# One exponential per graph with a copied head, the sum scaled from PSUM, moments behind the output, and programs without loops

## The chip, the cores and the metric

The kernel runs on one core of a Trainium2 chip. The metric is the device time in microseconds. The core has five programs that run side by side and meet by semaphores: TensorE (PE), VectorE (DVE), ScalarE (ACT), GpSimd (POOL) and SyncE (SP), which issues nearly all DMAs.

## The reference

x holds 128 graphs of 128 nodes and 512 features; all share one 128 x 128 adjacency. Cut to what matters:

```python
# layer 0
h = maximum(layernorm(x), 0)
A = einsum('od,bdn->bon', adj, h);  C = A + b0[:, None]
x = x + max over the last axis of relu(A[:, :, None, :] + (C - A)[:, :, :, None])
# layer 1
h = maximum(layernorm(x), 0)
q, k, v = h @ Wq + bq, h @ Wk + bk, h @ Wv + bv          # 8 heads of 64
scores = q k^T / 8 + (-1e9 where adj == 0)
x = x + softmax(scores) @ v
```

In layer 0, C - A is b0 for every element, so the term per node is relu(max over features of A + b0): one number per graph and node, the column c. It is added to a whole row of x, so the layer norm of layer 1 is the same as that of the input, and one h serves both layers. The result is x + c + softmax(scores) v, with bv added to x, since the weights of a softmax sum to one.

## The kernel before

To keep float32 precision with float16 matmuls, each operand is split: a "head" in float16 and a "rest", the float16 of the difference. Each product is three matmuls (head x head, head x rest, rest x head).

The unit of work is a slot: in slot k every engine works on one graph in each of its steps, at offsets that are constants at the top of the file (lines 25 to 27). The order inside a slot is written out by hand, per engine, in functions named slot:

- SP: loads x of graph k+8 (L175), transposes h of graph k+5 by DMA (L198), stores y of graph k-7 (L180), transposes the probabilities of graph k-5 by DMA (L206).
- GpSimd: adds bv (L277) and the column c (L280) to x of graph k; the rest of h of graph k+5 (L268); the rest of one chunk of q or k (L289); four small operations for scale and shift of the layer norm of graph k+6 (norm_scales, L247 to L257), which wait for VectorE's moments; the rest of the probabilities of graph k-5 (L296); the rest of the second chunk (L289).
- ScalarE: the head of v (L352); the column c of graph k (L374); h of graph k+5 in float32 and float16 (L333, L334); a chunk of q or k as head and in float32 (L345, L347); two exponentials of graph k-5 (L362 into float16, L364 into float32); the second chunk.
- VectorE: for graph k-5 the masked scores (L451), the row maximum (L455) and the shift (L458); the maximum over the adjacency product of graph k+3 (L435); the rest of v of graph k-1 (L440); the statistics of graph k+6 (L417); for graph k-7 the reciprocal of the row sums (L465), its scaling (L467) and eight outputs of y (L474); the aggregate of the statistics (L427).
- TensorE: scores of graph k-5 (L660), two chunks of q or k for a group of four graphs (L631), the adjacency product of graph k+4 (L616), v of graph k (L643), probabilities x v of graph k-6 (L675).

The PSUM tile o_ps of the last product has one copy: L675 waits until y of the graph before is done (`wait(pe, y_done, m)`). So does the pair of score banks, for masked. Five graphs are left for a tail, in which VectorE alternates between shift and output (L598 to L604).

SP's program is written out for all 128 slots. The other four have eight slots straight, a loop of 14 rounds of eight slots, and eight straight:

Of the kernel before, what the change touches and what calls it, by code (L numbers as in the profile page):

```python
# [6 lines left out]
ALU = mybir.AluOpType  # L7
ACT = mybir.ActivationFunctionType
# [5 lines left out]
P = 128  # L14
# [7 lines left out]
EXP_BITS = 0x7F800000  # L22
UP_BITS = float((2 * 127 + 14) << 23)
PEAK_FLOOR = 2.0 ** -32
LOAD_AHEAD, MOMENTS_AHEAD, NORM_AHEAD, TURN_AHEAD, PREP_AHEAD, AMAX_AHEAD = 8, 6, 5, 5, 4, 3
ATTN_BEHIND, OUT_BEHIND, STORE_BEHIND = 5, 6, 7
V_BEHIND, Y_BEHIND = 1, 7
DVE_RESTS = 3
# [2 lines left out]
def graph_layers(nc, x, adj, b0, wq, bq, wk, bk, wv, bv, out):  # L31
# [6 lines left out]
    with ExitStack() as ctx:  # L38
        def sb(name, shape, dt=F32):
            return ctx.enter_context(nc.sbuf_tensor(name, shape, dt))  # L40
# [20 lines left out]
        up = sb("up", [P, 4])  # L61
        down = sb("down", [P, 4])
        undo = sb("undo", [P, 3])
        redo = sb("redo", [P, 2])
        score_scale = sb("score_scale", [P, 1])
        peak_floor = sb("peak_floor", [P, 4])
        bqk_peak = sb("bqk_peak", [P, 2])
# [4 lines left out]
        plus_minus = sb("plus_minus", [P, 2])  # L72

        x_in = sb("x_in", [P, RING, D])
        xbv = sb("xbv", [P, D])
        x1 = sb("x1", [P, RING, D])
        y = sb("y", [P, 2, D])
        stats = sb("stats", [P, 2, 6])
# [16 lines left out]
        probs = sb("probs", [P, H, P])  # L95
        probs16 = sb("probs16", [P, 2, 2, H, P], F16)
        probsT = sb("probsT", [P, 2, 2, H, P], F16)
        inv_sum = sb("inv_sum", [P, 2, H // 2])
        out_scale = sb("out_scale", [P, 2, H // 2])


# [26 lines left out]
            sem("s_ready"), sem("masked_done"), sem("max_done"), sem("shifted_done"), sem("probs_done"))  # L128
        probs_head_done, probs_rest_done = sem("probs_head_done"), sem("probs_rest_done")
        probsT_done = [sem(f"probsT_done{i}") for i in range(2)]  # L130
        o_ready, inv_sum_done, out_scale_done, y_done = sem("o_ready"), sem("inv_sum_done"), sem("out_scale_done"), sem("y_done")
        c_done, xc_done, x1_done = sem("c_done"), sem("xc_done"), sem("x1_done")

        def wait(eng, s, count):
# [19 lines left out]

        def slots(eng, slot, after_first=None):

            for k in range(RING):
                slot(0, k)
                if k == 0 and after_first:
                    after_first()  # L160
            with eng.Fori(RING, B - 2 * RING + 1, RING) as base:
                for k in range(RING):
                    slot(base, k)
            for k in range(RING):
                slot(B - RING, k)

        block = ctx.enter_context(nc.Block())

# [1 line left out]
        def _(sp):  # L170
            def load(base, k):
                if in_range(base, k):

                    wait(sp, x1_done, base + k - RING + 1)
                    sp.dma_start(x_in[:, k % RING, :], x[base + k, :, :]).then_inc(x_loaded[k % RING], 16)  # L175

            def store(base, k):
# [50 lines left out]
        def _(pool):  # L228
# [39 lines left out]
                    pool.tensor_tensor(h16[:, k % 4, 1, :], h32[:, k % 2, :], h16[:, k % 4, 0, :],  # L268
                                       ALU.subtract).then_inc(h_rest_done, 1)

            def add_c(base, k):

                if in_range(base, k):
                    m = base + k
                    wait(pool, y_done, m - RING + 1)
                    wait(pool, x1_done, m)
                    pool.tensor_tensor(xbv[:, :], x_in[:, k % RING, :], bv_rows[:, :], ALU.add).then_inc(xc_done, 1)  # L277
                    pool.wait_ge(xc_done, m + 1)
                    pool.wait_ge(c_done, m + 1)
                    pool.tensor_tensor(x1[:, k % RING, :], xbv[:, :],  # L280
                                       c_col[:, k % RING, :].to_broadcast([P, D]), ALU.add).then_inc(x1_done, 1)

            def qk_rest(base, k, u):

# [22 lines left out]

            def slot(base, k):
                u = 2 * (k % GROUP)
                add_c(base, k)  # L310
                rest(base, k + NORM_AHEAD)
                qk_rest(base, k, u)
                norm_scales(base, k + MOMENTS_AHEAD)
                probs_rest(base, k - ATTN_BEHIND)
                qk_rest(base, k, u + 1)

            slots(pool, slot)
            for graph in TAIL:
# [3 lines left out]
        def _(act):  # L322
# [33 lines left out]
            def exps(base, k):  # L356

                if in_range(base, k):
                    m = base + k
                    act.wait_ge(shifted_done, m + 1)  # L360
                    wait(act, probsT_done[k % 2], (m - k % 2) * 8)
                    nc.scalar.activation(probs16[:, k % 2, 0, :, :], shifted[:, :, :], ACT.Exp, scale=HD ** -0.5).then_inc(probs_head_done, 1)  # L362
                    wait(act, probs_rest_done, m)
                    nc.scalar.activation(probs[:, :, :], shifted[:, :, :], ACT.Exp, scale=HD ** -0.5).then_inc(probs_done, 1)  # L364

            def c_of(base, k):

                if in_range(base, k):
                    m = base + k
                    if isinstance(base, int) and m == 0:  # L370
                        act.wait_ge(down_done, 1)
                    act.wait_ge(a_evac, m + 1)
                    wait(act, x1_done, m - RING + 1)
                    nc.scalar.activation(c_col[:, k % RING, :], a_max[:, k % RING, :], ACT.Relu, scale=down[:, 3:4],  # L374
                                         bias=b0_col[:, :]).then_inc(c_done, 1)

            def w_head(j, batch):
                act.wait_ge(scale_done, batch + 1)
# [18 lines left out]
            def slot(base, k):  # L397
                u = 2 * (k % GROUP)
                v_head(base, k - 1)
                c_of(base, k)  # L400
                normalise(base, k + NORM_AHEAD)
                qk_out(base, k, u)
                exps(base, k - ATTN_BEHIND)
                qk_out(base, k, u + 1)

            slots(act, slot, after_first=lambda: w_head(1, 3))
            v_head(B, -1)
# [4 lines left out]
        def _(dve):  # L412
# [24 lines left out]
            def v_rest(base, k):  # L437
                if in_range(base, k):
# [3 lines left out]
                        proj[:, V_BANK, :].rearrange("p (h d) -> p h d", d=HD), P_SCALE,  # L442
                        v16[:, 0, k // GROUP % 2, k % GROUP, :, 0:HD], ALU.mult, ALU.subtract).then_inc(v_evac, 1)

            def softmax_shift(base, k, banks=sc):

                if in_range(base, k):
                    m = base + k
                    wait(dve, shifted_done, m)
                    dve.wait_ge(s_ready, m + 1)  # L450
                    nc.vector.scalar_tensor_tensor(masked[:, :, :], banks[:, :, :].rearrange("p t (h n) -> p (t h) n", n=P),  # L451
                                                   score_scale[:, :], mask8[:, :].unsqueeze(1).to_broadcast([P, H, P]),
                                                   ALU.mult, ALU.add).then_inc(masked_done, 1)
                    dve.wait_ge(masked_done, m + 1)
                    nc.vector.tensor_reduce(row_max[:, :], masked[:, :, :], AX.X, ALU.max).then_inc(max_done, 1)  # L455
                    dve.wait_ge(max_done, m + 1)
                    wait(dve, probs_done, m)
                    nc.vector.tensor_tensor(shifted[:, :, :], masked[:, :, :],  # L458
                                            row_max[:, :].unsqueeze(2).to_broadcast([P, H, P]), ALU.subtract).then_inc(shifted_done, 1)

            def attention_out(base, k):
                if in_range(base, k):
                    m = base + k
                    dve.wait_ge(o_ready, m + 1)
                    nc.vector.reciprocal(inv_sum[:, :, :], o_view[:, :, :, HD]).then_inc(inv_sum_done, 1)  # L465
                    dve.wait_ge(inv_sum_done, m + 1)
                    nc.vector.tensor_scalar(out_scale[:, :, :], inv_sum[:, :, :], undo[:, 2:3], None,  # L467
                                            ALU.mult).then_inc(out_scale_done, 1)
                    dve.wait_ge(out_scale_done, m + 1)
                    dve.wait_ge(x1_done, m + 1)  # L470
                    wait(dve, y_stored[k % 2], (m - k % 2) * 8)
# [41 lines left out]
            def projection_scales(j, i):  # L513
                dve.wait_ge(down_done, i + 1)
                nc.vector.tensor_scalar(undo[:, j:j + 1], down[:, j:j + 1], 1.0 / P_SCALE, None, ALU.mult).then_inc(undo_done, 1)
                if j < 2:
                    dve.wait_ge(scale_done, i + 1)
                    nc.vector.tensor_scalar(redo[:, j:j + 1], up[:, j:j + 1], H_SCALE * P_SCALE, None, ALU.mult).then_inc(redo_done, 1)
                    dve.wait_ge(redo_done, j + 1)
                    nc.vector.tensor_scalar(bqk_up[:, j, :], bqk[:, j, :], redo[:, j:j + 1], None, ALU.mult).then_inc(bias_done, 1)  # L520

            def w_rest(j, i):
# [55 lines left out]
            projection_scales(1, 3)  # L578
            dve.wait_ge(mask_done, 2)
            dve.wait_ge(undo_done, 3)  # L580

            def k_rest():

# [4 lines left out]
            def slot(base, k):  # L588
                softmax_shift(base, k - ATTN_BEHIND)
                if not isinstance(base, int) or base + k > 0:  # L590
                    adjacency_out(base, k + AMAX_AHEAD)
                v_rest(base, k - V_BEHIND)
                stats_of(base, k + MOMENTS_AHEAD)
                moments_wait(base, k + MOMENTS_AHEAD)
                attention_out(base, k - Y_BEHIND)
                moments_of(base, k + MOMENTS_AHEAD)

            slots(dve, slot, after_first=k_rest)  # L598
            v_rest(B, -V_BEHIND)
            for i, graph in enumerate(TAIL):  # L600
                softmax_shift(*graph, TAIL_BANKS[i % 3])
                attention_out(B, graph[1] - Y_BEHIND + ATTN_BEHIND)
            for k in range(-Y_BEHIND + ATTN_BEHIND, 0):
                attention_out(B, k)  # L604
# [145 lines left out]
```

## Time and profile before

| | |
|---|---|
| median of 3 runs | 1386.8 us (1386.61 to 1387.9) |
| the profiled execution | 1386.83 us |
| its span, first to last instruction | 1384.9 us |
| mean granted TensorE clock | 0.980 of full speed |
| busy: PE, DVE, ACT, POOL | 94%, 77%, 64%, 90% |
| DMA | 171.71 MB, mean 124 GB/s |
| stretch from 200 to 400 us | PE busy 194.42 us, DVE 157.31, ACT 131.52, POOL 188.33 |

Busy is the time in which an engine has an instruction in work; an instruction that is held up once it has begun counts as busy too. In the trace, a row of the timeline says when an instruction started, how long it took, and in brackets how long its engine had been idle before it and for whom.

### The profile page before, as it was taken

How to read it: one execution, taken by the hardware profiler on the slowest of the kernel's cores; microseconds unless marked ns; L12 is line 12 of the kernel's file. 1: busy time of each engine (PE TensorE's matmuls, PEld its weight loads, DVE VectorE, ACT ScalarE, POOL GpSimd, SP SyncE). 2: the span in 40 equal slices, each digit the busy share in tenths (PEclk: the TensorE clock that was granted, in tenths of full speed). 3: DMA queues.
4: the chain of work that ended last, by engine and by line, in shares of the span. 5: the costliest groups of instructions: out<-in, count | busy, mean ns of one | idle time of the engine just before them, and what ended most of it. 6: DMA issues, size and time to landing. Idle time of an engine off the chain costs nothing.

```text
span 1384.9 us, 32665 instructions
## 1 busy us (share of the span) xinstructions
PE 1304.8 (94%) x11145; PEld 676.4 (49%) x11145; DVE 1066.9 (77%) x2228; ACT 879.7 (64%) x1294; POOL 1242.3 (90%) x1288
## 2 busy tenths in 40 slices
PE   4899999999999999999999999999999999999982
PEld 1344545545455555545545455454545555455542
DVE  6458787787887887887887877878877878878777
ACT  4566666666666676666666666666766666666552
POOL 2888999999999999999999999999999999999852
PEclk8999999999999999999999999999999999999995
DMA  7244555555555565555555555555555555555445
GB/s 199 62 81 111 137 127 124 129 127 129 123 129 136 115 130 129 127 122 136 129 118 132 124 129 126 129 132 118 129 131 123 130 131 125 118 136 122 97 81 129
DMA packets 441378, 171.71 MB, mean 124 GB/s; under 512 B 406784, under 2 KB 406912, under 8 KB 441344
## 3 DMA queue, kind: packets, MB, share of 16 engines
q1 hardware_dynamic: 440000, 171.03, 55.3%
q10 hardware_dynamic: 1344, 0.27, 0.1%
q8 instruction: 16, 0.26, 0.1%
q14 instruction: 18, 0.15, 0.0%
HBM read 37.03 MB, written 33.55 MB: 51 GB/s over the span
## 4 chain that ended last, share of the span: by engine, by line
PE 75%; DVE 18%; issue 4%; DMA 1%; SPq 0%; DVEq 0%; POOL 0%; ACT 0%; POOLq 0%; ACTq 0%
PE proj L631 38%; PE proj L643 19%; PE sc L660 7%; PE o_ps L675 7%; PE proj L616 4%; DVE y L474 4%; DVE masked L451 3%; DVE row_max L455 3%; DVE out_scale L467 2%; DVE a_max L435 1%; DVE stats L417 1%; DVE v L440 1%; DVE inv_sum L465 1%; DMA x_in<-in_x 0%; DVE shifted L458 0%
## 5 line engine op out<-in xcount | busy, mean ns | idle before, releaser
L631 PE MATMUL proj<-hT,w 128*128 128x512 f16 x3072 | 689.8, 381 | 11.3 <-DMA hT<-h 6.8
L631 PEld LDWEIGHTS proj<-hT,w 128*128 128x128 f16 x3072 | 291.2, 98 | 361.0 <-issue 17.5
L643 PE MATMUL proj<-w,hT 128*128 128x512 f16 x1536 | 352.4, 379 | 1.1 <-DVE w L526 1.1
L451 DVE SCALAR_TENSOR_TENSOR masked<-sc,score_scale,mask 128x1024 f32<-128x1024 f32 x125 | 160.4, 1283 | 241.2 <-PE sc L660 241.2
L289 POOL TENSOR_TENSOR qkT<-qk,qkT 128x512 f16<-128x512 f32 x256 | 296.5, 1158 | 9.4 <-ACT qk L347 9.2
L296 POOL TENSOR_TENSOR probs<-probs 128x1024 f16<-128x1024 f32 x128 | 273.3, 2135 | 25.2 <-ACT probs L364 25.2
L345 ACT ACTIVATE qkT<-proj,bqk_up 128x512 f16<-128x512 f32 x256 | 173.4, 677 | 170.7 <-PE proj L631 170.7
L277 POOL TENSOR_TENSOR xbv<-x_in,bv_rows 128x512 f32<-128x512 f32 x128 | 276.2, 2158 | 0.0
L643 PEld LDWEIGHTS proj<-w,hT 128*128 128x128 f16 x1536 | 150.0, 98 | 182.8 <-DVE w L526 1.5
L474 DVE SCALAR_TENSOR_TENSOR y<-o_ps,out_scale,x 128x64 f32<-128x64 f32 x1024 | 208.2, 276 | 11.2
L458 DVE TENSOR_TENSOR shifted<-masked,row_max 128x1024 f32<-128x1024 f32 x128 | 189.2, 1478 | 4.4
L333 ACT ACTIVATE h<-x_in,h_add,h_mul 128x512 f32<-128x512 f32 x128 | 104.0, 813 | 110.6 <-POOL h_add L257 110.6
L347 ACT ACTIVATE qk<-proj,bqk_up 128x512 f32<-128x512 f32 x256 | 173.5, 678 | 0.0
L352 ACT ACTIVATE v<-proj 128x512 f16<-128x512 f32 x128 | 76.4, 597 | 151.1 <-PE proj L643 151.1
L362 ACT ACTIVATE probs<-shifted 128x1024 f16<-128x1024 f32 x128 | 135.3, 1057 | 48.3 <-DVE shifted L458 45.8
L675 PE MATMUL o_ps<-v,probsT 128*128 128x65 f16 (+1 forms) x3072 | 117.9, 195 | 45.3 <-DVE y L474 30.9
L455 DVE TENSOR_REDUCE row_max<-masked 128x8 f32<-128x1024 f32 x128 | 156.2, 1220 | 4.4
L675 PEld LDWEIGHTS o_ps<-v,probsT 128*128 128x128 f16 x3072 | 109.1, 99 | 85.9 <-issue 64.5
L268 POOL TENSOR_TENSOR h<-h 128x512 f16<-128x512 f32 x125 | 146.4, 1172 | 4.1 <-ACT h L334 4.1
L280 POOL TENSOR_TENSOR x<-xbv,c_col 128x512 f32<-128x512 f32 x128 | 133.8, 1045 | 10.9 <-ACT c_col L374 1.1
L364 ACT ACTIVATE probs<-shifted 128x1024 f32<-128x1024 f32 x128 | 133.2, 1041 | 0.0
L660 PE MATMUL sc<-qkT 64*128 64x128 f16 x3000 | 106.1, 218 | 5.5 <-DVE masked L451 5.5
(59 smaller groups left out, 937.6 us busy)
## 6 DMA issues: line engine op xcount, KB each, us to landing
x_in<-in_x SPq DMA_DIRECT2D x128, 256.0 KB, 2.6
out_x<-y SPq DMA_DIRECT2D x128, 256.0 KB, 2.3
hT<-h SPq DMA_TRANSPOSE x128, 3.1
probsT<-probs SPq DMA_TRANSPOSE x128, 4.3
w_raw<-in_L_gnn_Wq SPq DMA_DIRECT2D x1, 1024.0 KB, 9.2
w_raw<-in_L_gnn_Wv SPq DMA_DIRECT2D x1, 1024.0 KB, 11.4
w_raw<-in_L_gnn_Wk SPq DMA_DIRECT2D x1, 1024.0 KB, 13.4
bv_rows<-in_L_gnn_bv ACTq DMA_DIRECT2D x1, 256.0 KB, 6.8
```

The lines of the kernel that those rows point to most:

```text
L277: pool.tensor_tensor(xbv[:, :], x_in[:, k % RING, :], bv_rows[:, :], ALU.add).then_inc(xc_done, 1)
L289: pool.tensor_tensor(qk_place(k, u, 1), qk32[:, u % 2, :], qk_place(k, u, 0), ALU.subtract).then_inc(qk_rest_done, 1)
L296: pool.tensor_tensor(probs16[:, k % 2, 1, :, :], probs[:, :, :], probs16[:, k % 2, 0, :, :], ALU.subtract).then_inc(probs_rest_done, 1)
L347: nc.scalar.activation(qk32[:, u % 2, :], place, ACT.Identity, scale=P_SCALE, bias=bias).then_inc(qk_evac, 1)
L451: nc.vector.scalar_tensor_tensor(masked[:, :, :], banks[:, :, :].rearrange("p t (h n) -> p (t h) n", n=P), score_scale[:, :], mask8[:, :]. ...
L455: nc.vector.tensor_reduce(row_max[:, :], masked[:, :, :], AX.X, ALU.max).then_inc(max_done, 1)
L458: nc.vector.tensor_tensor(shifted[:, :, :], masked[:, :, :], row_max[:, :].unsqueeze(2).to_broadcast([P, H, P]), ALU.subtract).then_inc(sh ...
L474: last = nc.vector.scalar_tensor_tensor(y[:, k % 2, cols], o_view[:, h // 4, h % 4, 0:HD], out_scale[:, h // 4, h % 4:h % 4 + 1], x1[:, k ...
L631: last = nc.tensor.matmul(proj[:, u % 2, :], w16[:, j, s, c, col * P:(col + 1) * P], hT[:, k // GROUP % 2, t, c, :, :].rearrange("p g n -> ...
L643: last = nc.tensor.matmul(proj[:, V_BANK, :], hT[:, k // GROUP % 2, s, c, k % GROUP, :], w16[:, 2, t, c, :], start=(c == 0 and i == 0), st ...
L660: last = nc.tensor.matmul(banks[:, half, c * P:(c + 1) * P], qkT[rows, k // GROUP % 2, s, 0, c, k % GROUP, :], qkT[rows, k // GROUP % 2, t ...
L675: last = nc.tensor.matmul(o_view[:, h // 4, h % 4, 0:w], probsT[:, k % 2, s, h % 2 * 4 + h // 2, :], v16[:, t, k // GROUP % 2, k % GROUP, ...
```

## The change

- ScalarE makes one exponential per graph, the float32 one. The float16 head of the probabilities is a copy on VectorE (probs_head), placed behind v_rest and ahead of attention_out; GpSimd's rest follows it as before.
- The row sums are first scaled from PSUM into SBUF and the reciprocal is taken of the scaled sums. Before, the reciprocal was taken from PSUM and scaled in SBUF.
- On VectorE statistics and aggregate (stats_of, moments_of) both stand behind attention_out.
- ScalarE adds the column c to x (add_c, an Identity activation with c as bias, into the new double tile xc), at the end of its slot; GpSimd's one pass (add_bv) adds bv, at the end of its slot.
- x is loaded 7 graphs ahead, and a load waits for xc and no longer for x1.
- All programs are written out for 128 slots, without a loop.

```diff
-LOAD_AHEAD, MOMENTS_AHEAD, NORM_AHEAD, TURN_AHEAD, PREP_AHEAD, AMAX_AHEAD = 8, 6, 5, 5, 4, 3
+LOAD_AHEAD, MOMENTS_AHEAD, NORM_AHEAD, TURN_AHEAD, PREP_AHEAD, AMAX_AHEAD = 7, 6, 5, 5, 4, 3
...
-            for k in range(RING):
+            for k in range(B):
                 slot(0, k)
                 if k == 0 and after_first:
                     after_first()
-            with eng.Fori(RING, B - 2 * RING + 1, RING) as base:
-                for k in range(RING):
-                    slot(base, k)
-            for k in range(RING):
-                slot(B - RING, k)
...
-                    wait(sp, x1_done, base + k - RING + 1)
+                    wait(sp, xc_done, base + k - RING + 1)
...
-            def add_c(base, k):
+            def add_bv(base, k):
 
                 if in_range(base, k):
                     m = base + k
                     wait(pool, y_done, m - RING + 1)
-                    wait(pool, x1_done, m)
-                    pool.tensor_tensor(xbv[:, :], x_in[:, k % RING, :], bv_rows[:, :], ALU.add).then_inc(xc_done, 1)
                     pool.wait_ge(xc_done, m + 1)
-                    pool.wait_ge(c_done, m + 1)
-                    pool.tensor_tensor(x1[:, k % RING, :], xbv[:, :],
-                                       c_col[:, k % RING, :].to_broadcast([P, D]), ALU.add).then_inc(x1_done, 1)
+                    pool.tensor_tensor(x1[:, k % RING, :], xc[:, k % 2, :], bv_rows[:, :], ALU.add).then_inc(x1_done, 1)
...
                 u = 2 * (k % GROUP)
-                add_c(base, k)
                 rest(base, k + NORM_AHEAD)
                 qk_rest(base, k, u)
                 norm_scales(base, k + MOMENTS_AHEAD)
                 probs_rest(base, k - ATTN_BEHIND)
                 qk_rest(base, k, u + 1)
+                add_bv(base, k)
...
                     act.wait_ge(shifted_done, m + 1)
-                    wait(act, probsT_done[k % 2], (m - k % 2) * 8)
-                    nc.scalar.activation(probs16[:, k % 2, 0, :, :], shifted[:, :, :], ACT.Exp, scale=HD ** -0.5).then_inc(probs_head_done, 1)
                     wait(act, probs_rest_done, m)
                     nc.scalar.activation(probs[:, :, :], shifted[:, :, :], ACT.Exp, scale=HD ** -0.5).then_inc(probs_done, 1)
...
+            def add_c(base, k):
+
+                if in_range(base, k):
+                    m = base + k
+                    act.wait_ge(c_done, m + 1)
+                    wait(act, x1_done, m - 1)
+                    nc.scalar.activation(xc[:, k % 2, :], x_in[:, k % RING, :], ACT.Identity, bias=c_col[:, k % RING, :]).then_inc(xc_done, 1)
...
                 qk_out(base, k, u + 1)
+                add_c(base, k)
...
+            def probs_head(base, k):
+
+                if in_range(base, k):
+                    m = base + k
+                    dve.wait_ge(probs_done, m + 1)
+                    wait(dve, probsT_done[k % 2], (m - k % 2) * 8)
+                    nc.vector.tensor_copy(probs16[:, k % 2, 0, :, :], probs[:, :, :]).then_inc(probs_head_done, 1)
...
-                    nc.vector.reciprocal(inv_sum[:, :, :], o_view[:, :, :, HD]).then_inc(inv_sum_done, 1)
-                    dve.wait_ge(inv_sum_done, m + 1)
-                    nc.vector.tensor_scalar(out_scale[:, :, :], inv_sum[:, :, :], undo[:, 2:3], None,
-                                            ALU.mult).then_inc(out_scale_done, 1)
+                    nc.vector.tensor_scalar(scaled_sum[:, :, :], o_view[:, :, :, HD], redo[:, 2:3], None,
+                                            ALU.mult).then_inc(sum_done, 1)
+                    dve.wait_ge(sum_done, m + 1)
+                    nc.vector.reciprocal(out_scale[:, :, :], scaled_sum[:, :, :]).then_inc(out_scale_done, 1)
...
                 v_rest(base, k - V_BEHIND)
+                probs_head(base, k - ATTN_BEHIND)
+                attention_out(base, k - Y_BEHIND)
                 stats_of(base, k + MOMENTS_AHEAD)
                 moments_wait(base, k + MOMENTS_AHEAD)
-                attention_out(base, k - Y_BEHIND)
                 moments_of(base, k + MOMENTS_AHEAD)
...
                 softmax_shift(*graph, TAIL_BANKS[i % 3])
+                probs_head(*graph)
                 attention_out(B, graph[1] - Y_BEHIND + ATTN_BEHIND)
```

## Rows read from the trace of the kernel before

**Rows 1.** The page, parts 1 and 2: busy time, and the granted clock in tenths.

```profile
PE 1304.8 (94%) x11145; PEld 676.4 (49%) x11145; DVE 1066.9 (77%) x2228; ACT 879.7 (64%) x1294; POOL 1242.3 (90%) x1288
...
PEclk8999999999999999999999999999999999999995
```

**Rows 2.** The chain that ended last, shares of the span by engine.

```profile
PE 75%; DVE 18%; issue 4%; DMA 1%; SPq 0%; DVEq 0%; POOL 0%; ACT 0%; POOLq 0%; ACTq 0%
```

**Rows 3.** Timeline (start us, us, engine, line, operation), TensorE: scores of slots 8, 18, 123.

```profile
108.09 0.84 PE L660 MATMUL sc<-qkT 64*128 64x128 f16 x24
...
718.21 0.85 PE L660 MATMUL sc<-qkT 64*128 64x128 f16 x24
...
1293.99 0.84 PE L660 MATMUL sc<-qkT 64*128 64x128 f16 x24
```

**Rows 4.** Timeline of slot 8, VectorE's scaling and GpSimd's rest of h.

```profile
115.15 1.16 POOL L268 TENSOR_TENSOR h<-h 128x512 f16<-128x512 f32 x1
...
115.18 1.15 DVE L467 TENSOR_SCALAR out_scale<-inv_sum,undo 128x8 f32<-128x8 f32 x1
```

**Rows 5.** Groups by line: count, busy us, mean ns, idle before.

```profile
L467 DVE TENSOR_SCALAR out_scale<-inv_sum,undo 128x8 f32<-128x8 f32 x128 | 57.6, 450 | 4.6
```

**Rows 6.** Timeline from one y to the next, 705 to 717 us, VectorE and TensorE.

```profile
705.59 1.63 DVE L474 SCALAR_TENSOR_TENSOR y<-o_ps,out_scale,x 128x64 f32<-128x64 f32 x8
...
707.36 0.89 PE L675 MATMUL o_ps<-v,probsT 128*128 128x65 f16 x24 [0.91 <-DVE y L474]
...
708.18 0.84 PE L660 MATMUL sc<-qkT 64*128 64x128 f16 x24
...
709.07 1.28 DVE L451 SCALAR_TENSOR_TENSOR masked<-sc,score_scale,mask 128x1024 f32<-128x1024 f32 x1 [1.77 <-PE sc L660]
...
710.39 1.22 DVE L455 TENSOR_REDUCE row_max<-masked 128x8 f32<-128x1024 f32 x1
...
711.64 1.39 DVE L458 TENSOR_TENSOR shifted<-masked,row_max 128x1024 f32<-128x1024 f32 x1
...
714.15 0.68 DVE L417 BATCH_NORM_STATS2 stats<-x_in 128x6 f32<-128x512 f32 x1
...
714.86 0.21 DVE L465 RECIPROCAL inv_sum<-o_ps 128x8 f32<-128x8 f32 x1
...
715.10 0.23 DVE L467 TENSOR_SCALAR out_scale<-inv_sum,undo 128x8 f32<-128x8 f32 x1
...
715.37 1.63 DVE L474 SCALAR_TENSOR_TENSOR y<-o_ps,out_scale,x 128x64 f32<-128x64 f32 x8
```

**Rows 7.** Timeline of the tail, first and last of five shifts.

```profile
1345.14 1.22 DVE L458 TENSOR_TENSOR shifted<-masked,row_max 128x1024 f32<-128x1024 f32 x1
...
1368.80 1.22 DVE L458 TENSOR_TENSOR shifted<-masked,row_max 128x1024 f32<-128x1024 f32 x1
```

**Rows 8.** Timeline of the same slot as rows 6, GpSimd.

```profile
710.79 1.15 POOL L289 TENSOR_TENSOR qkT<-qk,qkT 128x512 f16<-128x512 f32 x1
...
711.91 2.25 POOL L277 TENSOR_TENSOR xbv<-x_in,bv_rows 128x512 f32<-128x512 f32 x1
```

**Rows 9.** Timeline of the slot before, shift and first exponential.

```profile
700.55 1.52 DVE L458 TENSOR_TENSOR shifted<-masked,row_max 128x1024 f32<-128x1024 f32 x1
...
702.18 1.06 ACT L362 ACTIVATE probs<-shifted 128x1024 f16<-128x1024 f32 x1 [0.25 <-DVE shifted L458]
```

**Rows 10.** Timeline of slot 5, from the aggregate to GpSimd's second rest.

```profile
84.83 0.18 DVE L427 BATCH_NORM_AGGREGATE mean_var<-stats 128x2 f32<-128x6 f32 x1
...
85.09 0.19 POOL L247 TENSOR_TENSOR var_eps<-mean_var,eps 128x1 f32<-128x1 f32 x1 [0.76 <-DVE mean_var L427]
...
86.40 2.13 POOL L296 TENSOR_TENSOR probs<-probs 128x1024 f16<-128x1024 f32 x1
...
88.48 1.17 POOL L289 TENSOR_TENSOR qkT<-qk,qkT 128x512 f16<-128x512 f32 x1
```

**Rows 11.** Timeline of the head, the mask.

```profile
9.79 0.19 DVE L551 TENSOR_SCALAR mask<-adj_sb 128x128 f32<-128x128 f32 x1
```

More of the change, by code:

```diff
@@ L63, in graph_layers @@
         undo = sb("undo", [P, 3])
-        redo = sb("redo", [P, 2])
+        redo = sb("redo", [P, 3])
         score_scale = sb("score_scale", [P, 1])
@@ L74, in graph_layers @@
         x_in = sb("x_in", [P, RING, D])
-        xbv = sb("xbv", [P, D])
+        xc = sb("xc", [P, 2, D])
         x1 = sb("x1", [P, RING, D])
@@ L97, in graph_layers @@
         probsT = sb("probsT", [P, 2, 2, H, P], F16)
-        inv_sum = sb("inv_sum", [P, 2, H // 2])
+        scaled_sum = sb("scaled_sum", [P, 2, H // 2])
         out_scale = sb("out_scale", [P, 2, H // 2])
@@ L130, in graph_layers @@
         probsT_done = [sem(f"probsT_done{i}") for i in range(2)]
-        o_ready, inv_sum_done, out_scale_done, y_done = sem("o_ready"), sem("inv_sum_done"), sem("out_scale_done"), sem("y_done")
+        o_ready, sum_done, out_scale_done, y_done = sem("o_ready"), sem("sum_done"), sem("out_scale_done"), sem("y_done")
         c_done, xc_done, x1_done = sem("c_done"), sem("xc_done"), sem("x1_done")
@@ L372, in c_of @@
                     act.wait_ge(a_evac, m + 1)
-                    wait(act, x1_done, m - RING + 1)
                     nc.scalar.activation(c_col[:, k % RING, :], a_max[:, k % RING, :], ACT.Relu, scale=down[:, 3:4],
                                          bias=b0_col[:, :]).then_inc(c_done, 1)
+            def add_c(base, k):
[4 more added lines that the diff above has]
+                    nc.scalar.activation(xc[:, k % 2, :], x_in[:, k % RING, :], ACT.Identity, bias=c_col[:, k % RING, :]).then_inc(xc_done, 1)
             def w_head(j, batch):
@@ L515, in projection_scales @@
                 nc.vector.tensor_scalar(undo[:, j:j + 1], down[:, j:j + 1], 1.0 / P_SCALE, None, ALU.mult).then_inc(undo_done, 1)
+                dve.wait_ge(scale_done, i + 1)
+                nc.vector.tensor_scalar(redo[:, j:j + 1], up[:, j:j + 1], H_SCALE * P_SCALE, None, ALU.mult).then_inc(redo_done, 1)
                 if j < 2:
-                    dve.wait_ge(scale_done, i + 1)
-                    nc.vector.tensor_scalar(redo[:, j:j + 1], up[:, j:j + 1], H_SCALE * P_SCALE, None, ALU.mult).then_inc(redo_done, 1)
-                    dve.wait_ge(redo_done, j + 1)
+                    dve.wait_ge(redo_done, i)
                     nc.vector.tensor_scalar(bqk_up[:, j, :], bqk[:, j, :], redo[:, j:j + 1], None, ALU.mult).then_inc(bias_done, 1)
@@ L580, in _ @@
             dve.wait_ge(undo_done, 3)
+            dve.wait_ge(redo_done, 3)
             def k_rest():
```

## The prediction

> **What bounds the kernel now.** I read the engine shares first, then the chain of waits, then the timeline of one slot on every engine. TensorE is busy 94% of the span and GpSimd 90% [rows 1], and three quarters of the chain lie on TensorE, 18% on VectorE [rows 2]. A share says nothing of who waits for whom, so the starts of the score matmuls give the length of a slot. An undisturbed one takes 718.21 - 708.18 = 10.03 us, in which TensorE's pieces stand end to end; but slots 8 to 122, 115 of them, take 1293.99 - 108.09 = 1185.9 us, 10.31 on average [rows 3]. 115 x 10.03 would be 1153.5, so 32.4 us are lost in stalls.
>
> The timeline shows where. In the first two slots of a loop round the small scaling of the inverse sums, L467, takes 1.15 instead of 0.23: it started at 115.18, GpSimd's subtraction at 115.15, and it ended with that [rows 4]. Over the run L467 sums to 57.6 us where 128 x 0.23 would be 29.4 [rows 5]; the rest, 28 us, is some 30 such waits. A lead of 0.03 us was enough for GpSimd to go first.
>
> A second fact is in the same slot. The outputs y end at 707.22; TensorE starts probs x v at 707.36, because the PSUM tile of the outputs has one copy, and the scores of the next slot at 708.18; VectorE masks at 709.07, takes the row maximum at 710.39, is ready to shift at 711.64, and its next y ends at 717.00 [rows 6]. That is a closed loop of 9.78 us from y to y, over VectorE and two TensorE pieces, only 0.25 below TensorE's 10.03. Whatever lengthens this loop beyond 10.03 is paid in each slot. I therefore lay the new order on this loop, with the old end of y as zero.
>
> And the shift L458 queues behind GpSimd too. It is alone at 1.22 [rows 7], but here it starts at 711.64, GpSimd's L289 runs until 711.94, and it ends at 713.03, 1.09 later. L277, dispatched at 711.91, ends 1.13 after the shift, at 714.16, for 2.25 in all [rows 6, 8]. So VectorE's two-input operation and its L467 take turns with GpSimd's instructions, whole instruction by whole instruction.
>
> The Trainium skill, "SBUF — State Buffer", section "Who interferes with whom", names this: VectorE and GpSimd share one pair of SBUF ports by an exclusive lock, and a VectorE instruction takes it with two SBUF inputs or in a 2-port mode (copy, cast, tensor_scalar). The rows above agree. By that rule the new copy takes the lock, a scaling from PSUM doesn't, and the reciprocal isn't in its list.
>
> **What goes.** The four programs written out: no loop rounds. The pattern of eight follows the rounds, and SP's program, straight already, holds nobody up, so I charge nothing for fetching; removing the stalls gives back at most the 32.4. L467 reads PSUM now and I take it as free of the turn-taking. GpSimd loses its second pass over x, not on the loop; ScalarE loses one exponential (1.06) and gains a pass over half as many elements, which I put below that; it is idle before the exponential [rows 9], so neither is on the loop. On SP's queue the load now goes by xc, made by ScalarE in the slot before, and no longer by x1; it is one graph less ahead, needed more than a slot later, and the transposes behind it are not held up: nothing. In the head an extra pass before the K weights stands in idle time: at most 1 us.
>
> **What comes, step by step (y ends at 0).** Moments: statistics now stand behind y and no longer before it. They start at -0.07, take 0.68, the aggregate follows at +0.03 and takes 0.18 [rows 6, 10]. GpSimd's first scale starts 0.08 later, at 0.90: 84.83 + 0.18 = 85.01 to 85.09. From it to probs_rest are 1.31, from there to the second qk_rest 2.08 [rows 10]. So qk_rest starts at 4.29 and ends at 5.44 (1.15, [rows 8]). The shift is ready at 4.42 (711.64 - 707.22). GpSimd is 0.13 ahead, more than the 0.03 that sufficed, so the shift ends at 5.44 + 1.09 = 6.53; it was 5.81. The statistics' 0.7 us are not hidden, they come back through GpSimd.
>
> Then the copy. The exponential starts 0.11 after the shift (702.07 to 702.18) and takes 1.06 [rows 9]; with 0.03 for the wait the copy is ready 1.20 after it, at 7.73. The maximum over the adjacency and v_rest fill until 1.12 after the shift [rows 6]. On GpSimd add_bv, dispatched at 5.41, has the shape of L277: it ends 1.13 after the shift, at 7.66, and h's rest, which is next in the program and has its inputs, is dispatched at 7.63. That is 0.10 ahead of the copy, and it runs 1.15, to 8.78.
>
> The copy's own length no row shows. One element per cycle is (1.22 - 0.68)/512 = 1.055 ns [rows 6, 7], 1.22 for 1024. At half of that, as the 128-element mask L551 suggests (0.19 us, where one element per cycle would be 0.68 - 384 x 1.055 ns = 0.275, [rows 11]), it is 0.66 alone and 0.54 + 0.02 = 0.56 after a wait. I take the half, and that it waits as L467 did, because both rows are of its kind (one SBUF source, SBUF destination). It ends at 9.34. The scaling starts at 9.32, the reciprocal 0.24 later, y 0.27 later, and takes 1.63 [rows 6]: y ends at **11.46**. Behind the waiting copy stand the scaling, the reciprocal, y and the next moments in VectorE's program; TensorE waits for that y, GpSimd for the moments.
>
> So the loop is 11.46 instead of 10.03. TensorE waits for y in each slot. Its granted clock stays at 2.4 GHz, I take it: it is at nine tenths or more in every slice but the first and last [rows 1], the long slots among them. The sum: 115 x 11.46 = 1317.9, against 1185.9: +132.0. In it -32.4 for the stalls and +164.5 for the loop. Slot 7 and the five slots behind 123, which have no moments to wait for, have a loop near 9.65 instead of 9.38: +2 together with the head.
>
> Tail: there four shifts take 23.66 us, from one end at 1346.36 to another at 1370.02 [rows 7]. Now the shift is followed by 1.20 until the copy, 0.60 (0.66 less the overlap with the next start), 0.24, 0.27, 1.54 (likewise), then mask, maximum and shift 1.32 + 1.25 + 1.22: 7.64, four times 30.6, +6.9. The last probs_rest starts some 0.3 earlier, as one copy replaces one exponential: +6.6.
>
> 1386.8 + 132.0 + 2 + 6.6 = **1527.4**. The profiled execution took 1386.83 outside a span of 1384.9, and the median is 1386.8, so nothing has to be scaled.
>
> **Bounds of what no row shows.** Copy: 0.56 with turn-taking, or 1.22 without: 7.73 + 1.22 + 2.11 gives a loop near 11.05. A copy that never has to wait and runs at half rate: 7.73 + 0.60 + 0.24 + 0.27 + 1.63 = 10.47, still above 10.03, as the 6.53 remains. Reciprocal from SBUF: free, or waiting for the qk_rest that starts at 9.34 (1.15): y ends about 12.2. The new pass on ScalarE: below nothing no, as it adds work; up to the 1.06 that goes it is covered. Written-out programs: between -32.4 and, if fetching should show, a few us.
>
> **Rivals.**
> (a) *One turn falls the other way.* If the shift gets ahead of qk_rest (0.13 apart), it ends at 5.64; qk_rest ends near 6.69, add_bv starts at 6.65, before the copy at 6.85, and ends 7.92; copy until 8.48, y at 10.6. Or the copy goes ahead of h's rest: 10.47. 115 x 10.55 = 1213, +27, with the tail about 1422. For it: both gaps are tenths. Against: 0.03 was enough elsewhere.
> (b) *The copy runs at one element a cycle:* 115 x 11.05 = 1271, +85: 1480.
> (c) *The reciprocal waits as L467 did:* 115 x 12.2 = 1403, +217: 1612. The skill's list leaves it out, and so do I.
> (d) *Not slower:* VectorE gets both turns as soon as it asks. The shift ends at 5.64, the copy at 7.45, y at 9.58: below 10.03, and TensorE sets the slot. 115 x 10.03 = 1153.5, -32.4, tail +6.6 and +2: 1363. It decides at a loop of 10.03. For it: GpSimd loses a pass and could lie earlier in the slot. Against: its second half starts from the moments, and these from y, so the spare time lies ahead of them.
> (e) *The change doesn't do what it says:* stalls come from elsewhere than the loop rounds and stay. That adds to any case up to 32 us: no case of its own.
>
> **How the numbers follow.** Forecast 0.52 (1500 to 1545), (a) 0.15, (b) 0.08, (c) 0.08, (d) 0.14, others 0.03. The time is the forecast's. The range leaves out (c) and (d): 1412 to 1548. A difference of 0.2%, 2.8 us, is what can be told from none. Slower: 0.84; faster: (d) and a little, 0.14; same 0.02.
>
> **What would show it.** Right: score starts some 11.4 apart in slots 8 to 122 with no pattern of eight; the shift at 2.1 (4.42 to 6.53); the copy at about 1.6 with GpSimd's h rest running beside its first two thirds; "probs x v waits for y" as TensorE's largest wait; GpSimd idle 1.5 us or more before its first scale; the small reciprocal at 0.2. Wrong: slots of 10.03, a shift of 1.2 to 1.5, or a copy of 0.66 that starts on its own time.

## The result, and the profile after

The changed kernel takes 1516.91 us (median of 4 runs, 1516.14 to 1517.54) against 1386.7 us for the kernel before: a ratio of 1.0937, 95% interval 1.0918 to 1.0956. It is slower by 130 us. The forecast was 1527, slower.

The page after, parts 1 and 2 (busy time, and the granted clock in tenths) and its chain by engine:

```profile
PE 1334.3 (88%) x11145; PEld 664.1 (44%) x11145; DVE 1297.3 (86%) x2357; ACT 837.1 (55%) x1294; POOL 1164.2 (77%) x1160
...
PEclk8999999999999999999999999999999999999995
...
DVE 59%; PE 19%; issue 17%; ACT 1%; DVEq 0%; DMA 0%; POOLq 0%; ACTq 0%
```

Against [rows 1, 2]: GpSimd fell from 90% to 77% busy, ScalarE from 64% to 55%, and the kernel is slower. The chain lay on TensorE for 75% and lies on VectorE for 59% now. The clock is unchanged (mean 0.982, 0.980 before). A kernel in which two loaded engines got lighter and the time grew has got a new loop of waits; the shares can't say which.

Timeline after, TensorE, the scores of slots 8 and 123:

```profile
109.83 0.84 PE L668 MATMUL sc<-qkT 64*128 64x128 f16 x24
...
1417.62 0.84 PE L668 MATMUL sc<-qkT 64*128 64x128 f16 x24
```

115 slots take 1307.8 us, 11.37 each, where the first and the last row of [rows 3] give 1185.9. (The middle row there, at 718.21, belongs to slot 67 and not to slot 18; the slot before it, 66, is the third of its loop round, and its 10.03 us stand.) That is +121.9. Up to slot 8 the span grew by 1.7, behind slot 123 by 7.2 (98.1 instead of 90.9). The three sum to 130.8, the difference of the spans (1515.7 - 1384.9).

Timeline after, one slot, VectorE with the first pieces of TensorE, GpSimd and ScalarE that matter to it (y of the slot before ends at 699.80 + 0.47 = 700.27):

```profile
699.80 0.47 DVE L479 SCALAR_TENSOR_TENSOR y<-o_ps,out_scale,x 128x64 f32<-128x64 f32 x2
...
700.18 0.68 DVE L414 BATCH_NORM_STATS2 stats<-x_in 128x6 f32<-128x512 f32 x1
...
700.41 0.89 PE L683 MATMUL o_ps<-v,probsT 128*128 128x65 f16 x24 [0.83 <-DVE y L479]
...
701.16 0.19 POOL L242 TENSOR_TENSOR var_eps<-mean_var,eps 128x1 f32<-128x1 f32 x1 [1.92 <-DVE mean_var L424]
...
702.47 2.14 POOL L287 TENSOR_TENSOR probs<-probs 128x1024 f16<-128x1024 f32 x1
...
704.57 1.16 POOL L280 TENSOR_TENSOR qkT<-qk,qkT 128x512 f16<-128x512 f32 x1
...
704.76 2.04 DVE L463 TENSOR_TENSOR shifted<-masked,row_max 128x1024 f32<-128x1024 f32 x1
...
705.68 2.25 POOL L272 TENSOR_TENSOR x<-xc,bv_rows 128x512 f32<-128x512 f32 x1
...
706.84 1.06 ACT L353 ACTIVATE probs<-shifted 128x1024 f32<-128x1024 f32 x1 [0.76 <-DVE shifted L463]
...
707.90 1.15 POOL L263 TENSOR_TENSOR h<-h 128x512 f16<-128x512 f32 x1
707.93 1.67 DVE L448 CAST probs<-probs 128x1024 f16<-128x1024 f32 x1
...
709.52 0.21 DVE L470 TENSOR_SCALAR scaled_sum<-o_ps,redo 128x8 f32<-128x8 f32 x1
709.77 0.20 DVE L473 RECIPROCAL out_scale<-scaled_sum 128x8 f32<-128x8 f32 x1
710.01 1.62 DVE L479 SCALAR_TENSOR_TENSOR y<-o_ps,out_scale,x 128x64 f32<-128x64 f32 x8
```

Read it against [rows 6, 8]. The shift is asked for at 704.76, 4.49 after the last y; GpSimd's L280 went at 704.57 and ends at 705.73; the shift ends at 706.80, after 2.04 instead of 1.39. The copy is asked for at 707.93, 0.03 after GpSimd's L263, waits until 709.05 and ends at 709.60. The next y ends at 711.63: 11.36 us after the last. GpSimd has stood idle for 1.92 us before L242, waiting for the moments.

Groups by line after (count, busy us, mean ns, idle before and its releaser):

```profile
L463 DVE TENSOR_TENSOR shifted<-masked,row_max 128x1024 f32<-128x1024 f32 x128 | 251.6, 1965 | 4.4
L448 DVE CAST probs<-probs 128x1024 f16<-128x1024 f32 x128 | 203.5, 1590 | 7.2 <-ACT probs L353 7.2
L473 DVE RECIPROCAL out_scale<-scaled_sum 128x8 f32<-128x8 f32 x128 | 26.0, 203 | 4.4
L242 POOL TENSOR_TENSOR var_eps<-mean_var,eps 128x1 f32<-128x1 f32 x128 | 24.7, 193 | 249.4 <-DVE mean_var L424 249.4
```

VectorE's idle time in front of shift and copy is 4.4 and 7.2 us in all 128 slots together, next to nothing. The waits for GpSimd are inside the instructions' own durations, so they look like work: of VectorE's 1297 busy us, some 210 (128 x (1.965 - 1.22) and 128 x (1.59 - 0.69)) are waiting.

### The profile page after: what moved, and what is told of

It is laid out like the page before. It is cut to its first block, busy times and chain, and to the rows that moved or that the text cites. A ratio compares the mean times of both kernels' runs of the same rounds, so it can differ in the third digit from the quotient of the medians.

```text
span 1515.7 us, 30498 instructions
## 1 busy us (share of the span) xinstructions
PE 1334.3 (88%) x11145; PEld 664.1 (44%) x11145; DVE 1297.3 (86%) x2357; ACT 837.1 (55%) x1294; POOL 1164.2 (77%) x1160
## 4 chain that ended last, share of the span: by engine, by line
DVE 59%; PE 19%; issue 17%; ACT 1%; DVEq 0%; DMA 0%; POOLq 0%; ACTq 0%
DVE y L479 13%; DVE probs L448 12%; DVE masked L456 10%; DVE row_max L460 10%; PE o_ps L683 7%; PE sc L668 6%; DVE a_max L432 5%; DVE v L437 5%; PE proj L639 3%; PE proj L651 2%; DVE out_scale L473 2%; DVE scaled_sum L470 1%; DVE shifted L463 1%; ACT probs L353 0%; PE proj L624 0%
## 5 line engine op out<-in xcount | busy, mean ns | idle before, releaser
L280 POOL TENSOR_TENSOR qkT<-qk,qkT 128x512 f16<-128x512 f32 x256 | 347.8, 1359 | 19.1 <-ACT qk L338 18.8
L272 POOL TENSOR_TENSOR x<-xc,bv_rows 128x512 f32<-128x512 f32 x128 | 276.5, 2160 | 0.0
L463 DVE TENSOR_TENSOR shifted<-masked,row_max 128x1024 f32<-128x1024 f32 x128 | 251.6, 1965 | 4.4
L242 POOL TENSOR_TENSOR var_eps<-mean_var,eps 128x1 f32<-128x1 f32 x128 | 24.7, 193 | 249.4 <-DVE mean_var L424 249.4
L448 DVE CAST probs<-probs 128x1024 f16<-128x1024 f32 x128 | 203.5, 1590 | 7.2 <-ACT probs L353 7.2
L683 PEld LDWEIGHTS o_ps<-v,probsT 128*128 128x128 f16 x3072 | 105.5, 99 | 178.9 <-issue 175.3
L263 POOL TENSOR_TENSOR h<-h 128x512 f16<-128x512 f32 x125 | 146.4, 1171 | 11.7 <-ACT h L324 8.3
L624 PE MATMUL proj<-h,adjT 128*128 128x512 f16 x372 | 100.2, 377 | 23.1 <-DVE a_max L432 23.0
```

Source lines behind the costliest of these rows:

```text
L272: pool.tensor_tensor(x1[:, k % RING, :], xc[:, k % 2, :], bv_rows[:, :], ALU.add).then_inc(x1_done, 1)
L280: pool.tensor_tensor(qk_place(k, u, 1), qk32[:, u % 2, :], qk_place(k, u, 0), ALU.subtract).then_inc(qk_rest_done, 1)
L448: nc.vector.tensor_copy(probs16[:, k % 2, 0, :, :], probs[:, :, :]).then_inc(probs_head_done, 1)
L463: nc.vector.tensor_tensor(shifted[:, :, :], masked[:, :, :], row_max[:, :].unsqueeze(2).to_broadcast([P, H, P]), ALU.subtract).then_inc(sh ...
L683: last = nc.tensor.matmul(o_view[:, h // 4, h % 4, 0:w], probsT[:, k % 2, s, h % 2 * 4 + h // 2, :], v16[:, t, k // GROUP % 2, k % GROUP, ...
```

## The experiments

Times are medians; the ratio stands beside each with its 95% interval, against runs of the kernel before on the same chip.

**The copy's turn: `a_spare_op`.** One operation of one element per partition is added on GpSimd, so that the copy is dispatched before the rest of h. (The new tile and its semaphore are not shown.)

```diff
                 u = 2 * (k % GROUP)
+                wait(pool, spare_done, k)
+                pool.tensor_tensor(spare[:, :], eps[:, :], eps[:, :], ALU.add).then_inc(spare_done, 1)
                 rest(base, k + NORM_AHEAD)
```

> The changed kernel with one operation more: GpSimd adds two columns of one element (0.2 us, its result unused) ahead of the rest of h in each slot. Theory (GpSimd's rest of h is dispatched 0.03 us ahead of VectorE's copy and so goes first): with 0.2 us more in front of it the copy goes first, takes 0.8 us and not 1.67, and a slot falls from 11.37 to about 10.4 us: 1400 to 1415 us, over 100 us faster by added work. Rival (the copy is slow by itself or by the traffic of both engines, not by a turn): the slot stays at 11.37 or grows by up to 0.2, 1515 to 1540 us.

Measured: 1406.54 us, ratio 1.013 (1.0114 to 1.0147). Added work took 110 us off the changed kernel. Its timeline:

```profile
709.72 0.18 POOL L303 TENSOR_TENSOR spare<-eps 128x1 f32<-128x1 f32 x1
709.74 0.71 DVE L451 CAST probs<-probs 128x1024 f16<-128x1024 f32 x1
709.86 1.60 POOL L264 TENSOR_TENSOR h<-h 128x512 f16<-128x512 f32 x1
```

Now the copy takes 0.71 and GpSimd's rest waits, 1.60 instead of 1.15. Nearly all slots are 10.39 to 10.42. The copy alone is short; what cost 1 us was being second by 0.03.

**Is it the turn or the length? `a_reduce_copy`.** The copy is made by an instruction that takes 1.22 us where the copy alone takes 0.69, but that was expected to take no turns: the row maximum, a reduction too, shows no waits.

```diff
-                    nc.vector.tensor_copy(probs16[:, k % 2, 0, :, :], probs[:, :, :]).then_inc(probs_head_done, 1)
+                    nc.vector.tensor_reduce(probs16[:, k % 2, 0, :, :], probs[:, :, :].unsqueeze(3), AX.X, ALU.max).then_inc(probs_head_done, 1)
```

> The changed kernel with the copy made by a reduction over an axis of one element, which gives the same values at one element a cycle. Theory (the reduction takes no turns with GpSimd, as the row maximum shows no waits): it takes 1.22 us instead of the copy's 0.69 alone, but starts at once and ends 2.35 us behind the shift and not 2.80; slot 10.9 us, 1460 to 1475 us: a slower instruction gives the faster kernel. Rival (any VectorE instruction of this size waits, or work alone counts): 0.5 us more per slot, 1570 to 1580 us.

Measured: 1469.51 us, ratio 1.0593 (1.0577 to 1.0609), slots of 10.92. Its timeline:

```profile
706.70 1.16 POOL L263 TENSOR_TENSOR h<-h 128x512 f16<-128x512 f32 x1
706.74 1.22 DVE L448 TENSOR_REDUCE probs<-probs 128x1024 f16<-128x1024 f32 x1
```

GpSimd is 0.04 ahead as before, and neither waits: 1.16 and 1.22 beside each other. The slower instruction is 47 us faster. So it is neither the length nor traffic, but a turn: the copy needs it and the reduction doesn't.

**The moments: `a_stats_behind_copy` and `a_stats_before_copy`.** The first puts the statistics back in front of the output, behind the copy; the second one place further, in front of the copy.

```diff
                 v_rest(base, k - V_BEHIND)
                 probs_head(base, k - ATTN_BEHIND)
-                attention_out(base, k - Y_BEHIND)
                 stats_of(base, k + MOMENTS_AHEAD)
                 moments_wait(base, k + MOMENTS_AHEAD)
+                attention_out(base, k - Y_BEHIND)
                 moments_of(base, k + MOMENTS_AHEAD)
```

> The changed kernel with the statistics back in front of the output (behind the copy), as they were before the change. Theory (what the moments' new place takes off VectorE's path, 0.7 us, comes back through GpSimd, whose scales, two rests and so the shift start that much later): the shift takes 1.39 and not 2.04 us, the statistics stand on the path instead, the slot is 11.3 us: 1505 to 1517 us, no difference to speak of. Rival (the later moments are a loss by themselves): 0.7 us per slot less, about 1435 us. Second rival (they are a gain): 0.7 us per slot more, about 1595 us.

Measured: 1517.4 us, ratio 1.0938 (1.0921 to 1.0955), against 1516.91 and 1.0937 for the changed kernel: no difference. The shift falls to 1.3 us, and the statistics stand on the path instead; slots of 11.37 in both. Its groups:

```profile
L463 DVE TENSOR_TENSOR shifted<-masked,row_max 128x1024 f32<-128x1024 f32 x128 | 167.8, 1311 | 4.4
L448 DVE CAST probs<-probs 128x1024 f16<-128x1024 f32 x128 | 203.7, 1591 | 7.2 <-ACT probs L353 7.2
```

The shift's mean is 1.31 us instead of 1.97, and the copy's is unchanged.

```diff
                 v_rest(base, k - V_BEHIND)
+                stats_of(base, k + MOMENTS_AHEAD)
+                moments_wait(base, k + MOMENTS_AHEAD)
                 probs_head(base, k - ATTN_BEHIND)
                 attention_out(base, k - Y_BEHIND)
-                stats_of(base, k + MOMENTS_AHEAD)
-                moments_wait(base, k + MOMENTS_AHEAD)
                 moments_of(base, k + MOMENTS_AHEAD)
```

> The changed kernel with the statistics in front of the copy. Theory (VectorE waits there for GpSimd's rest of h anyway, so 0.68 us of statistics cost nothing in that place, and the moments come 0.7 us earlier): the shift ends 5.8 us after y and not 6.5, the copy still ends 2.8 us behind the shift and takes about 1.0, the slot is 10.64 us: 1428 to 1438 us. Rival (the copy's wait is no wait for a turn but its own length): the copy still takes 1.67 us, the slot is 11.3 us and the time above 1500 us.

Measured: 1432.57 us, ratio 1.0327 (1.0311 to 1.0343), slots of 10.64. Its timeline:

```profile
710.56 1.16 POOL L263 TENSOR_TENSOR h<-h 128x512 f16<-128x512 f32 x1
710.59 0.68 DVE L414 BATCH_NORM_STATS2 stats<-x_in 128x6 f32<-128x512 f32 x1
711.30 0.97 DVE L448 CAST probs<-probs 128x1024 f16<-128x1024 f32 x1
```

The same three instructions in another order. The statistics run in the time in which the copy could not start anyway, and the copy takes 0.97 us instead of 1.67. The moments are early as well.

**Without the copy: `a_two_exps`.** The whole change, but the head from a second exponential. (The copy goes in the tail too, not shown.)

```diff
                     act.wait_ge(shifted_done, m + 1)
+                    wait(act, probsT_done[k % 2], (m - k % 2) * 8)
+                    nc.scalar.activation(probs16[:, k % 2, 0, :, :], shifted[:, :, :], ACT.Exp, scale=HD ** -0.5).then_inc(probs_head_done, 1)
...
-                probs_head(base, k - ATTN_BEHIND)
```

> The changed kernel, with the head of the probabilities made by a second exponential on ScalarE as before, and no copy on VectorE; the rest of the change stays. Theory (y to y is a loop over VectorE, and the copy's 2.8 us behind the shift, of them 1.1 a turn behind GpSimd, is what lifts it over 10.03): the shift still takes 2.0 us, y ends 3.2 us behind it, the loop is 9.8 us and TensorE sets slots of 10.03: 1353 to 1360 us. Rival (the moments behind the output are the larger part of the loss): the time stays above 1420 us.

Measured: 1374.43 us, ratio 0.9903 (0.9887 to 0.992). An exponential in the copy's place takes 142 us off, more than the whole loss, so the moments behind the output were not the larger part of it. But the expected 1353 to 1360 were missed. The slots come as 10.03, 10.03, 10.53. Its timeline in the third:

```profile
712.18 1.16 POOL L280 TENSOR_TENSOR qkT<-qk,qkT 128x512 f16<-128x512 f32 x1
713.30 1.27 POOL L272 TENSOR_TENSOR x<-xc,bv_rows 128x512 f32<-128x512 f32 x1
713.45 2.20 DVE L465 TENSOR_TENSOR shifted<-masked,row_max 128x1024 f32<-128x1024 f32 x1
...
716.40 0.81 PE L624 MATMUL proj<-h,adjT 128*128 128x512 f16 x3 [0.34 <-DVE a_max L434]
```

With a short loop TensorE sets the slot, VectorE's shift is asked for later after y (5.56 us here, 4.49 in the changed kernel), and GpSimd gets in a second instruction, the addition of bv, 0.15 ahead. The shift ends late, and TensorE waits 0.34 us for the PSUM bank that the maximum behind it reads and 0.19 for that of v_rest, which is the length that the slot has grown by. I had laid the loop with TensorE waiting for y and missed what changes when it doesn't.

**The kernel before, one part each: `b_written_out` and `b_sum_psum`.**

```diff
-            for k in range(RING):
+            for k in range(B):
                 slot(0, k)
                 if k == 0 and after_first:
                     after_first()
-            with eng.Fori(RING, B - 2 * RING + 1, RING) as base:
...
```

> The kernel before with its four looped programs written out and nothing else. Theory (the stalls of the kernel before are turns lost to GpSimd, started by VectorE's 0.2 us delay in the first slots of a loop round): the pattern of eight goes, slots 8 to 122 take 10.03 to 10.09 us, the scaling of the inverse sums 0.23 us in nearly all of them, time 1354 to 1362 us. Rival (VectorE drifts against GpSimd by itself, some 0.05 us per slot, and the rounds have no part in it): the pattern stays and so does the time, 1380 to 1390 us.

Measured: 1361.6 us, ratio 0.9808 (0.9792 to 0.9825). The pattern of eight is gone; most slots take 10.08. GpSimd's instructions stand end to end there (of the 800 us from 400 to 1200 it is busy for 775), and about 1.1 of L272's 2.25 us are its wait for the shift:

```profile
707.35 2.25 POOL L272 TENSOR_TENSOR xbv<-x_in,bv_rows 128x512 f32<-128x512 f32 x1
...
709.68 1.04 POOL L275 TENSOR_TENSOR x<-xbv,c_col 128x512 f32<-128x512 f32 x1
...
710.55 0.23 DVE L462 TENSOR_SCALAR out_scale<-inv_sum,undo 128x8 f32<-128x8 f32 x1
710.68 1.16 POOL L263 TENSOR_TENSOR h<-h 128x512 f16<-128x512 f32 x1
```

The small scaling is 0.13 ahead of GpSimd and does not lose its turn here; over the run it takes 31.9 us instead of 57.6.

```diff
-                    nc.vector.reciprocal(inv_sum[:, :, :], o_view[:, :, :, HD]).then_inc(inv_sum_done, 1)
+                    nc.vector.tensor_scalar(inv_sum[:, :, :], o_view[:, :, :, HD], redo[:, 2:3], None,
+                                            ALU.mult).then_inc(inv_sum_done, 1)
                     dve.wait_ge(inv_sum_done, m + 1)
-                    nc.vector.tensor_scalar(out_scale[:, :, :], inv_sum[:, :, :], undo[:, 2:3], None,
-                                            ALU.mult).then_inc(out_scale_done, 1)
+                    nc.vector.reciprocal(out_scale[:, :, :], inv_sum[:, :, :]).then_inc(out_scale_done, 1)
```

(How `redo` gets its third column, before the first slot, is not shown.)

> The kernel before, with its loops, but the row sums scaled from PSUM first and the reciprocal taken of the scaled sums. Theory (the scaling waits its turn behind GpSimd because source and destination are in SBUF; from PSUM it does not, and the reciprocal does not either): both small operations take 0.2 us in every slot, some 28 us go although the loops stay, 1356 to 1364 us. Rival (the loop round itself costs the 2.3 us, the wait is only where it shows): no gain, 1383 to 1390 us.

Measured: 1364.32 us, ratio 0.9826 (0.981 to 0.9842), 0.3 us above the range that was expected. Its groups, to set beside [rows 5]:

```profile
L465 DVE TENSOR_SCALAR inv_sum<-o_ps,redo 128x8 f32<-128x8 f32 x128 | 28.8, 225 | 17.3 <-DVE stats L417 7.8 <-PE o_ps L676 6.4
L468 DVE RECIPROCAL out_scale<-inv_sum 128x8 f32<-128x8 f32 x128 | 26.0, 203 | 4.4
```

With the loops in place the two small operations take 28.8 + 26.0 us instead of 26.4 + 57.6 (L465 and L467 of the kernel before), 29 less; the round still costs some 0.65 us (10.14, 10.27 and 10.33 in place of three 10.03). Each of the two parts removes 24 to 26 us. Both together would be 50, more than the 32.4 that were lost in stalls, so their gains can't add: they are two cures of one ill. No run has the two and nothing else.

**Turns asked for: `best_turn`, `best_no_turn`, `a_turns`.** best_turn keeps the written-out programs, the scaling from PSUM and the column on ScalarE, has two exponentials and the statistics in front of the output, and one wait more on GpSimd:

```diff
             def add_bv(base, k):
...
+                    wait(pool, shifted_done, m - ATTN_BEHIND + 2)
                     wait(pool, y_done, m - RING + 1)
```

> Of the change there stay: programs written out, sums scaled from PSUM, ScalarE adding the column. The head of the probabilities comes from a second exponential again, the statistics stand in front of the output as before, and GpSimd waits for the shift before it adds bv. Theory (the loop from y to y must stay below 10.03 us; GpSimd has 1 to 2 us of spare time in a slot, and the one turn that must not go wrong is that of the shift): slots of 10.03 us without a pattern, 1353 to 1358 us, below the 1361.6 us of the kernel before with its programs written out. Rival (GpSimd's wait makes it late for its own chain): slots above 10.1 us, 1362 us or more.

Measured: 1354.18 us, ratio 0.9768 (0.9755 to 0.9782), every slot 10.03. Its interval lies below that of b_written_out.

best_no_turn is the same without that line.

> The fastest version so far without GpSimd's wait for the shift; nothing else differs. Theory (with TensorE setting the slot, VectorE asks for its shift some 0.05 to 0.1 us after GpSimd may dispatch the addition of bv, so every second slot or so GpSimd goes first and the shift and y come 0.9 us late): a pattern of 10.03 and about 10.6 us, shifts of 2.2 us among those of 1.2 to 1.5, 1375 to 1395 us. Rival (the wait does nothing, GpSimd's lighter load alone gives the 10.03): 1353 to 1358 us.

Measured: 1397.31 us, ratio 1.0065 (1.0047 to 1.0083); slots of 10.03 and 10.75 by turns, and 2 us above the expected range. One wait, with no work taken away, is worth 43 us here and decides between 2.3% faster and 0.7% slower than the kernel before. Two shifts in a row in it:

```profile
703.90 1.27 POOL L272 TENSOR_TENSOR x<-xc,bv_rows 128x512 f32<-128x512 f32 x1
703.97 2.28 DVE L465 TENSOR_TENSOR shifted<-masked,row_max 128x1024 f32<-128x1024 f32 x1
...
714.71 1.32 DVE L465 TENSOR_TENSOR shifted<-masked,row_max 128x1024 f32<-128x1024 f32 x1
714.90 2.26 POOL L272 TENSOR_TENSOR x<-xc,bv_rows 128x512 f32<-128x512 f32 x1
```

0.07 behind GpSimd the shift takes 2.28, in the next slot 0.19 ahead of it 1.32.

a_turns is the whole change with nothing taken out and two waits on GpSimd:

```diff
+                wait(pool, shifted_done, k - ATTN_BEHIND + 2)
                 qk_rest(base, k, u + 1)
+                wait(pool, probs_head_done, k - ATTN_BEHIND + 2)
                 add_bv(base, k)
```

> The whole change kept, one exponential and copy included, with two waits on GpSimd: the second rest of q and k waits for the shift, and the addition of bv waits for the copy. Nothing else is taken out. Theory (the change's loss is two lost turns, 0.9 us at the shift and 1.0 at the copy, not its work): the shift takes 1.2, the copy 0.7 to 0.8 us, y ends 9.5 to 9.7 us after the last y, below 10.03; GpSimd, which now waits in the middle of its slot, is nearly full: slots of 10.03 to 10.2 us, and a tail 7 us longer than that of the kernel before: 1361 to 1380 us. Rival (the copy's work on VectorE is too much even without waits): slots above 10.4 us, 1405 us or more.

Measured: 1362.34 us, ratio 0.9822 (0.9805 to 0.9838), all slots but one 10.03. Its timeline:

```profile
702.96 1.22 DVE L465 TENSOR_TENSOR shifted<-masked,row_max 128x1024 f32<-128x1024 f32 x1
...
704.27 1.16 POOL L280 TENSOR_TENSOR qkT<-qk,qkT 128x512 f16<-128x512 f32 x1 [1.30 <-DVE shifted L465]
...
705.31 0.69 DVE L450 CAST probs<-probs 128x1024 f16<-128x1024 f32 x1
...
706.08 1.28 POOL L272 TENSOR_TENSOR x<-xc,bv_rows 128x512 f32<-128x512 f32 x1 [0.66 <-DVE probs L450]
```

GpSimd now stands idle twice, 1.30 and 0.66 us per slot, and the kernel is 155 us faster than the changed one. The change's work fits in the slot; its order did not. What each of the two waits gives alone was not run.

## Why the prediction was right

The mechanism held at each step, and one size was a little off. One step held by a margin so small that part of it is luck.

- *The loop from y to y decides, not the shares.* Forecast 11.46 us, measured 11.36. Shown by four runs on the changed kernel, whose slots were worked out from the loop beforehand as 10.4, 10.64, 10.9 and 11.3 and came as 10.40, 10.64, 10.92 and 11.37. Busy time gives no such order: a_spare_op has 20 us more of GpSimd and takes 110 us less, and a_stats_behind_copy has 84 us less of VectorE and takes as long.
- *The moments come back through GpSimd.* The shift was to end 6.53 after y, and it did (700.27 to 706.80). That the move is worth nothing in either direction is shown by a_stats_behind_copy, 1517.4.
- *The copy goes second.* Forecast to be ready at 7.73 and to end at 9.34; it was ready at 7.66 and ended at 9.33. The exponential started 0.04 and not 0.11 behind the shift, so the lead that decided was 0.03 and not 0.10. Had VectorE asked first, by however little, the result would probably have been some 110 us lower, as in a_spare_op and rival (a): in the second slot of a_two_exps VectorE's shift asked 0.04 ahead of GpSimd's L272 (703.42, 703.46), took 1.23 us and left the wait to GpSimd, 2.32. My working of the two requests was off by 0.07, more than the lead that decided. That the copy came second was therefore in part luck.
- *Copy at half the time per element, reciprocal free.* The copy took 0.69 alone and 0.55 after its wait (0.66 and 0.56 forecast), and the reciprocal 0.202 to 0.204 in every slot. Rivals (b) and (c) are out.
- *The mis-sized term:* from the copy's end to y's end I summed 2.12 us and it is 2.03, because the scaling starts 0.08 ahead of the copy's end and y 0.24, not 0.27, behind the reciprocal. 115 x 0.09 is the 10 us between 1527 and 1517.
- *Head and tail:* +1.7 and +7.2, 8.9 together, where +2 for the head and the last slots and +6.6 for the tail were forecast, 8.6 together.
- *The stalls of the loop rounds:* taking out the rounds was to give back at most 32.4; b_written_out shows 26, as its slots are 10.08 and not 10.03 (115 x 0.05 is the other 6). So the stalls go with the loop rounds, and rival (e) is out. In the changed kernel this gain doesn't show by itself: 115 x (11.37 - 10.03) = 154 us went to the loop.
- *TensorE's clock:* the stretch from 200 to 400 us, after, has the granted clock at 1.00, with TensorE busy for 182.59 of 200 us:

```profile
200.00:400.00 200.00, 182.59 (x1551) 90.95 (x1551) 177.00 (x312) 113.14 (x176) 162.30 (x160) 1.00 0.52 115
```

Here the columns are length, busy PE, PEld, DVE, ACT, POOL, granted clock, DMA share, GB/s. So idle gaps of 0.83 us in each slot did not lower it.

Rival (d), VectorE getting each turn when it asks, is refuted as a description of the change, but a_turns shows its number was right: 1363 forecast for it, 1362.3 measured once the turns are asked for.

What the prediction lacked is the case in which TensorE sets the slot: then requests fall at other places, and a turn that was safe is lost (a_two_exps, best_no_turn). What stays open: the gain of each part alone in best_turn (column on ScalarE, scaling from PSUM) was not separated.

## What to carry to other kernels

When two engines take turns, lay the new order on the loop that sets the slot and compare the times at which each asks; a lead of 0.03 us decides over 1 us per slot, so such a lead is luck and should be replaced by a wait, even one that leaves the other engine idle. An instruction that waits for its turn shows as busy: compare its duration with its shortest in the trace before calling the engine loaded. Moving work off a loop helps only if nothing that starts behind it comes back into the loop.

## What the runs showed of the hardware that was not expected

- A GpSimd operation of 0.18 us in front of another decides which engine goes first for 1.2 us: VectorE's request during the small one is served before GpSimd's next (709.72, 709.74 and 709.86 in a_spare_op).
- A reduction over an axis of one element copies 1024 float32 elements per partition to float16 in 1.22 us with no turn to wait for; the copy takes 0.69 alone and 1.67 when it is second.
- A strict alternation of 10.03 and 10.75 us slots can come from turns alone (best_no_turn), and, as its timeline reads, a period of three (a_two_exps), in programs without any loop. One wait more made the first even at 10.03 (best_turn).
